# An RWKV recurrence with its products in fp16 high and low parts, and part of its vector work moved to ScalarE and GpSimd

## The reference

```python
low = jnp.tanh((x + delta * mu_x) @ W_x1).reshape(B, T, 5, PROJ_LR)
mus = jnp.einsum('blnr,dnr->blnd', low, W_x2) + x_bias
xr, xw, xk, xv, xg = [x + delta * mus[:, :, i] for i in range(5)]
r = (xr @ W_r)...; k = (xk @ W_k)...; v = (xv @ W_v)...; g = xg @ W_g
w = -jnp.exp(jnp.tanh(xw @ W_w1) @ W_w2 + b_w2)
def step(S, inp):
    o_t = jnp.einsum('bhk,bhkv->bhv', r_t, S) + jnp.einsum('bhk,hk,bhk,bhv->bhv', r_t, u, k_t, v_t)
    S = jnp.exp(w_t)[..., None] * S + k_t[..., :, None] * v_t[..., None, :]
o = ((o - mean) * jax.lax.rsqrt(var + EPS)).reshape(B, T, VAL_DIM)
o = (o * gn_w + gn_b) * (g * jax.nn.sigmoid(g))
return o @ W_o
```

## Time and profile before

| | |
|---|---|
| three runs | 1841.08, 1846.48, 1845.13 us |
| median | 1845.13 us |
| the profiled execution | 1845.41 us, of which 1843.6 us are its span |
| busy in the span | PE 1734.1, DVE 1442.4, ACT 1408.9, POOL 1431.1 us |
| mean granted clock of PE | 0.976 of full speed |

### The profile page before, as it was taken

The page is one execution under the profiler, slowest core; times in us unless marked ns, Lnnn a source line. Parts: engine busy times, 40 slices in busy tenths (PEclk is TensorE's granted clock), DMA queues, the critical chain, the costliest instruction groups (busy, mean ns, idle before and its releaser), DMA issues. The chain is left out here.

```text
span 1843.6 us, 54099 instructions
## 1 busy us (share of the span) xinstructions
PE 1734.1 (94%) x22920; PEld 1099.5 (60%) x22920; DVE 1442.4 (78%) x2658; ACT 1408.9 (76%) x1737; POOL 1431.1 (78%) x851
## 2 busy tenths in 40 slices
PE   5999999999999999999999999987899999978997
PEld 2466666666666666666666666675566666653454
DVE  5888888888888888888888887535888888855785
ACT  2688888888888888888888888943898888853464
POOL 6699999999999999999999999974765566634122
PEclk9899999999999999999999999998999999989999
DMA  5101010101011010101010100041111111100000
GB/s 141 27 20 31 19 31 22 28 25 29 24 27 26 25 31 19 31 23 28 23 31 19 28 20 9 2 157 29 40 41 37 37 37 37 33 25 2 1 0 23
DMA packets 71080, 57.02 MB, mean 31 GB/s; under 512 B 29196, under 2 KB 64184, under 8 KB 70840
## 3 DMA queue, kind: packets, MB, share of 16 engines
q1 hardware_dynamic: 70840, 53.57, 11.5%
HBM read 14.67 MB, written 1.05 MB: 9 GB/s over the span
## 5 line engine op out<-in xcount | busy, mean ns | idle before, releaser
L278 POOL TENSOR_TENSOR ah_probs_lo<-ah_probs,ah_probs_hi 128x1024 f16<-128x1024 f32 x512 | 1073.2, 2134 | 78.0 <-ACT ah_probs L487 77.9
L542 DVE TENSOR_REDUCE ah_part_max<-ah_p_m 128x1 f32<-128x512 f32 x1024 | 668.5, 685 | 121.5 <-PE ah_p_m L342 111.2
L484 ACT ACTIVATE ah_probs_hi<-ah_p_s 128x1024 f16<-128x1024 f32 x512 | 530.9, 1037 | 189.6 <-PE ah_p_s L358 178.4
L487 ACT ACTIVATE ah_probs<-ah_p_s 128x1024 f32<-128x1024 f32 x512 | 531.3, 1038 | 0.0
L372 PE MATMUL ah_p_o<-ah_v_hi,ah_probs_hi 128*128 128x65 f16 x4096 | 470.6, 195 | 5.7 <-POOL ah_probs_lo L278 5.1
L374 PE MATMUL ah_p_o<-ah_v_lo,ah_probs_hi 128*128 128x64 f16 x4096 | 470.6, 193 | 0.0
L376 PE MATMUL ah_p_o<-ah_v_hi,ah_probs_lo 128*128 128x65 f16 x4096 | 470.3, 194 | 0.0
L372 PEld LDWEIGHTS ah_p_o<-ah_v_hi,ah_probs_hi 128*128 128x128 f16 x4096 | 383.0, 98 | 84.4 <-DVE a_attn L565 12.2
L374 PEld LDWEIGHTS ah_p_o<-ah_v_lo,ah_probs_hi 128*128 128x128 f16 x4096 | 378.5, 98 | 91.3
L342 PE MATMUL ah_p_m<-ah_k_hi_lo,ah_q_hi_twice 128*128 128x512 f16 x1024 | 393.8, 385 | 6.6 <-DVE ah_part_max L542 3.5
L357 PE MATMUL ah_p_s<-ah_q_hi_twice,ah_k_hi_lo 128*128 128x512 f16 x1024 | 388.6, 380 | 0.8 <-ACT ah_probs L487 0.4
(11 more groups left out here) (316 smaller groups left out, 3083.4 us busy)
## 6 DMA issues: line engine op xcount, KB each, us to landing
ba_v_skew<-ba_v_own SPq DMA_DIRECT2D x64, 129.0 KB, 2.3
ah_q_hi_twice<-ah_hi SPq DMA_DIRECT2D x128, 64.0 KB, 2.0
ah_k_hi_lo<-ah_hi SPq DMA_DIRECT2D x64, 64.0 KB, 1.9
ah_one_k_hi<-ah_hi SPq DMA_DIRECT2D x64, 64.0 KB, 2.0
ah_k_hi_lo<-ah_lo SPq DMA_DIRECT2D x64, 64.0 KB, 2.0
ah_max_q_lo<-ah_lo SPq DMA_DIRECT2D x64, 64.0 KB, 2.0
ah_w_head<-in_w_heads SPq DMA_DIRECT2D x16, 160.0 KB, 2.5
bw_rot<-in_rot SPq DMA_DIRECT2D x4, 512.0 KB, 10.6
```

What stands on the lines that cost most here:

```text
L278: pool.tensor_tensor(pl[:, p % RW, :, :], pb[:, p % RP, :, :], ph[:, p % RW, :, :], ALU.subtract).then_inc(lo_pool, 1)
L484: act.activation(ph[:, p % RW, :, :], p_s[:, p % 2, :, :], ACT.Exp, scale=HD ** -0.5)
L487: act.activation(pb[:, p % RP, :, :], p_s[:, p % 2, :, :], ACT.Exp, scale=HD ** -0.5).then_inc(exp_done, 1)
L542: dve.tensor_reduce(part[:, t, 2 * half + b:2 * half + b + 1], p_m[:, b, :], AX, ALU.max).then_inc(maxed, 1)
```

## The change

- *Products.* The inputs of r, k and v are split into an f16 high part (ACT, `high_x`) and an f16 rest (POOL, `low_x`, into the memory of hT); so are the weights (POOL, four instructions ahead of the recurrence). A product is three f16 products into one bank: high by high, high by rest, rest by high. The tanh for the decay is made twice by weights laid out twice: the lower 64 partitions hold the high part, the upper 64 become the rest (`low_tw`, DVE), so that w takes two f16 products.
- *Splits.* `low_x` of chunk 0 stands in the mixing part, that of chunk c + 1 in the steps h = 0, 1, 2 of chunk c, each ahead of that step's bonus.
- *Bonus.* u*k*v is made by ACT (a copy with a factor per partition), added by POOL (`bonus`), and POOL makes the carry copy. DVE's scan takes its first value straight from the last column of the chunk before. DVE multiplies by r one step later (`weigh`), and so PE makes r(n - 1) and out(n - 2) in step n.
- *Norm of the outputs.* The mean is taken off within `out` (other constants in sel). ACT copies and squares (`centre`). The root is the exponential of minus half a logarithm, with one Newton step by DVE (four small instructions); logarithm and exponential are in one table, loaded once.
- *Places.* `turn_o` of a chunk moves from h = 3 of the next chunk to h = 0 of the one after it; `scale_o` and `norm_o` likewise to h = 0, `gate_o` to h = 1, `ln_root` to h = 3.

```diff
-                    pe.matmul(p_w[:, :], ww2[:, rs], tw[:, tok(c)], start=True, stop=True).then_inc(w_ready, 1)
+                    pe.matmul(p_w[:, :], w2_hi[:, rs], tw[:, tok(c)], start=True, stop=False)
+                    pe.matmul(p_w[:, :], w2_lo[0:P // 2, rs], tw[0:P // 2, tok(c)], start=False,
+                              stop=True).then_inc(w_ready, 1)
...
+                def three(out, k, n, ready):
+                    c, h = divmod(n, HCH)
+                    rs = slice(h * P, (h + 1) * P)
+                    pe.matmul(out, w_hi[:, k, rs], x_hi[:, k, tok(c)], start=True, stop=False)
+                    pe.matmul(out, w_hi[:, k, rs], x_lo[:, k, tok(c)], start=False, stop=False)
+                    pe.matmul(out, w_lo[:, k, rs], x_hi[:, k, tok(c)], start=False, stop=True).then_inc(ready, 1)
...
+                    three(p_kr[:, 0, :], K_COL, n, k_ready)
                     if n >= 1:
-                        out(n - 1)
-                    if h == 3 and c >= 1:
-                        turn_o(c - 1)
+                        receive(n - 1)
+                    if n >= 2:
+                        out(n - 2)
+                    if h == 0 and c >= 2:
+                        turn_o(c - 2)
                     if h == 1 and c >= 2:
                         out_y(c - 2)
+                receive(STEPS - 1)
+                out(STEPS - 2)
+                turn_o(CLAST - 1)
                 out(STEPS - 1)
...
+                    act.wait_ge(kv_done, n + 1)
...
+                    act.activation(ukv[:, n % 2, :], kv[:, n % 2, :], ACT.Copy,
+                                   scale=scols[:, 1, h:h + 1]).then_inc(ukv_done, 1)
+                    if h == 0 and c >= 2:
+                        scale_o(c - 2)
                     if h == 0 and c == CLAST:
                         norm(1, 0)
-                    if h == 1 and c >= 1:
-                        square(c - 1)
                     if h == 2 and c >= 1:
+                        centre(c - 1)
+                    if h == 3 and c >= 1:
                         root(c - 1)
...
+                for n in range(STEPS):
+                    c, h = divmod(n, HCH)
+                    if h == 0 and c >= 2:
+                        norm_o(c - 2)
+                    if h == 1 and c >= 2:
                         gate_o(c - 2)
-                    norm_o(c - 1)
-                    if c >= 2:
+                    if h < 3 and c < CLAST:
+                        low_x(c + 1, 2 - h)
+                    bonus(n)
+                    if c < CLAST:
+                        carry(n)
+                    if h == 3 and c >= 2:
                         ln_root(1, c - 2)
+                norm_o(CLAST - 1)
```

More of the change, by code:

```diff
@@ L1791, in _ @@
                 pe.wait_ge(z_ready, NCH)
[L1792 removed]
+                pe.wait_ge(w_lo_done, 2)
+                pe.wait_ge(tw_f32_done, NCH)
+                pe.wait_ge(tmp_ready, MIXES * NCH)
                 for n in range(STEPS):
@@ L1951, in _ @@
                 copy_x2(0)
-                square(CLAST)
+                centre(CLAST)
+                root(CLAST)
                 tanh_f(0, 0)
-                root(CLAST)
                 tanh_f(0, 1)
@@ L1999, in mix, with low_x, bonus, carry @@
                     pool.tensor_tensor(mixed_x, tmp[:, n % 2, :], xTp[:, xtok(c)], ALU.add).then_inc(mixed, 1)
+                def low_x(c, k):
+                    pool.wait_ge(mixed, MIXES * (c + 1))
+                    pool.wait_ge(x_hi_done, 3 * (c + 1))
+                    pool.tensor_tensor(x_lo[:, k, tok(c)], (x_r, x_k, x_v)[k][:, tok(c)], x_hi[:, k, tok(c)],
+                                       ALU.subtract).then_inc(x_lo_done, 1)
+                def bonus(n):
+                    c, h = divmod(n, HCH)
+                    pool.wait_ge(scanned, n + 1)
+                    if c >= 1:
+                        pool.wait_ge(carried, n - HCH + 1)
+                    if n >= 2:
+                        pool.wait_ge(pr_done, n - 1)
+                    pool.wait_ge(ukv_done, n + 1)
+                    pool.tensor_tensor(m[:, n % 2, :], ukv[:, n % 2, :], st[:, h, c % 2, 0:CH],
+                                       ALU.add).then_inc(m_done, 1)
+                def carry(n):
+                    c, h = divmod(n, HCH)
+                    pool.tensor_copy(st[:, h, (c + 1) % 2, 0:1], st[:, h, c % 2, CH:CH + 1]).then_inc(carried, 1)
                 def norm_o(c):
@@ L2019, in _ @@
                 pool.wait_ge(cleared, 2)
-                for c in range(NCH - 1):
-                    ln_root(0, c)
+                ln_root(0, 0)
+                ln_root(0, 1)
+                pool.wait_ge(late.scan_in, late.SCAN)
+                pool.tensor_copy(w_hi[:, :, :], w[:, :, :]).then_inc(w_hi_done, 1)
+                pool.tensor_copy(w2_hi[:, :], ww2[:, :]).then_inc(w_hi_done, 1)
+                ln_root(0, 2)
                 for c in range(NCH):
@@ L2147, in _ @@
                         if i == 2 and c >= 1:
+                            low_tw(c - 1)
                             gate_g(c - 1)
@@ L2153, in _ @@
                         delta_z(c + 2)
+                low_tw(CLAST)
                 gate_g(CLAST)
@@ L2193, in _ @@
                     dve.tensor_tensor(pr[:, n % 2, :], m[:, n % 2, :], p_kr[:, 1, :], ALU.mult).then_inc(pr_done, 1)
+                for n in range(STEPS):
+                    c, h = divmod(n, HCH)
+                    dve.wait_ge(v_done, n + 1)
+                    dve.wait_ge(k_ready, n + 1)
+                    if n >= 2:
+                        dve.wait_ge(ukv_done, n - 1)
+                    dve.tensor_tensor(kv[:, n % 2, :], p_kr[:, 0, :], v_sb[:, n % 2, :], ALU.mult).then_inc(kv_done, 1)
+                    dve.wait_ge(kv_done, n + 1)
+                    dve.wait_ge(dec_done, n + 1)
+                    first = st[:, h, 0, 0:1] if c == 0 else st[:, h, (c - 1) % 2, CH:CH + 1]
+                    dve.tensor_tensor_scan(st[:, h, c % 2, 1:], dec[:, n % 2, :], kv[:, n % 2, :], first, ALU.mult,
+                                           ALU.add).then_inc(scanned, 1)
+                    if n >= 1:
+                        weigh(n - 1)
                     if n == 0:
```

171 lines of the change are left out of this document (93 added, 78 removed).

## The result

The changed kernel takes 1849.62 us (median of 8 runs, 1847.89 to 1852.53) against 1846.42 for the kernel before (8 runs, 1841.08 to 1848.03). The ratio is 1.0023, with a 95% interval from 1.0013 to 1.0033: slower by a little, and within the 0.3% set as the bound. 1849 was predicted.

What follows compares the result with a forecast made beforehand. PE (TensorE) was taken to bound the recurrence at 4.33 us a step, with DVE close behind. The terms -8.4 + 2.7 + 0.9 + 3.6 + 3.4 + 1.3 = +3.5 us gave 1849 us, range 1836 to 1858.

Steps and rivals of the forecast that it cites:

- TensorE in chunks 0 and 1: Recurrence, first two chunks: f16 products cut most steps to 3.2 us, 26.65 against 35.01, minus 8.4 us.
- Chunks 2 and 3: Recurrence, last two chunks: three slower chains, 39.25 against 36.53 us, plus 2.7, and plus 0.9 for half-speed products.
- (a): Step 8: norm_o, transposes and scale_o of chunk 0 delay the next exponential and v; 4.1 us instead of 3.2.
- (b): Step 9: gate_o of chunk 0, behind the bonus and held by a scan, delays out_y and w; 6.05 us.
- (c): Step 12: statistics, ln_root, norm_o, transposes, scale_o, norm, exponential and v in a chain; the step takes 8.8 us.
- Mixing: Mixing of the inputs: low_tw, subtractions and f16 copies delay the first kv by 3.6 us; bounds 0.7 and 5.
- Tail: After the last pr: transposes ahead of the last out, and ACT work ahead of the first tanh; plus 3.4 and 1.3 us.
- The 3.4: Tail: chunk 2's transposes ahead of the last out make last pr to first gate product 7.35 us, from 3.97.
- the 1.3: Tail: ACT does centring, root and table load ahead of the first tanh; plus 1.3 us, bounds 0 and 2.
- the chains don't bind: First rival, chunk ends: they arrive in time, chunks 2 and 3 run like 0 and 1; 1837 us, chance 0.28.
- Half clock: Second rival, recurrence: PE's waits halve its clock, 6.3 us a step; two or three give 1855 to 1858; chance 0.18.
- scan and POOL exclude each other: Third rival, recurrence: steps with a subtraction take 3.7 us instead of 3.2, plus 4.5, 1853 us; chance 0.10.

Runs made afterwards that it cites:

- f32_products: The changed kernel with v, k and r each made by one f32 product again, splits made but not read; ratio 1.0040 to the kernel before.
- mixing_order: The changed kernel with low_tw behind all parts, one low_x moved a chunk later, and chunk 3's f16 copies ahead of the gate's tanh; ratio 0.9990 to the kernel before.
- all_moves: The changed kernel with the edits of both_moves, tail_order and mixing_order together; 1838.97 us, ratio 0.9951 to the kernel before.
- both_moves: The changed kernel with the edits of norm_late and norm_o_first together; ratio 0.9993 to the kernel before.
- norm_late: The changed kernel with only ACT's norm of tokens 0 moved from step 12 to behind the root of step 15; ratio 1.0007 to the kernel before.
- norm_o_first: The changed kernel with only POOL's norm_o of chunks 0 and 1 moved ahead of ln_root, to the end of h = 3; ratio 0.9988 to the kernel before.
- all_y_f32: all_y_later with v, k and r each made by one f32 product again; 1843.29 us, ratio 0.9985 to the kernel before.
- tail_order: The changed kernel with, behind step 15, chunk 2's norm_o ahead of ln_root and scale_o ahead of norm; ratio 1.0010 to the kernel before.
- bonus_on_dve: The changed kernel with the bonus back on DVE as one instruction, without ACT's copy and POOL's addition; ratio 1.0074 to the kernel before.
- all_y_later: all_moves with out_y of chunks 0 and 1 one step later and low_tw of two chunks behind the last gate; 1832.78 us, ratio 0.9923 to the kernel before.
- low_x_twice: The changed kernel with each low_x of the loop done once more into a tile nothing reads; ratio 1.0043 to the kernel before.

## Why the prediction came out right

*TensorE in chunks 0 and 1 (26.65 predicted, 27.16 measured).* Right in mechanism for the steps at PE's pace, and f32_products shows it. The step was mis-sized by 0.2: w's two products start 0.32 apart, not 0.22. The first step is shorter (2.54, it has no r and no out). That h = 2 took 3.96 (3.9) is luck. The prediction put the copy and the square of the outputs on ACT; in the trace DVE has no gap in this step (chosen rows of step 6):

```profile
1741.93 1.16 POOL L2056 TENSOR_TENSOR t_hT<-t_x_r,t_x_rkv_hi 128x512 f16<-128x512 f32 x1
1742.04 2.14 DVE L2270 TENSOR_TENSOR_SCAN t_state<-t_decay,t_state,t_kv 128x512 f32<-128x512 f32 x1
1744.19 0.60 ACT L1983 ACTIVATE t_v<-t_p_v 128x512 f32<-128x512 f32 x1
1744.68 0.67 DVE L2177 TENSOR_REDUCE t_ssq<-t_sq 128x64 f32<-128x512 f32 x1
1745.27 0.67 DVE L2266 TENSOR_TENSOR t_kv<-t_p_kr,t_v 128x512 f32<-128x512 f32 x1
```

The subtraction holds the scan, the sum of squares (0.6), which the prediction left out of DVE's work, stands behind it, and v was there at 1744.79, 0.48 ahead of kv(7). Where the same scan took 1.66 and 1.65 us (mixing_order, all_moves), the step took 3.52 and 3.51. h = 3 took 3.99 instead of 3.55, because the first operation of the Newton step takes 0.91 us while POOL adds the bonus, not 0.2 (0.18 in the tail, where POOL rests):

```profile
1747.18 0.66 DVE L2258 TENSOR_TENSOR t_pr<-t_m,t_p_kr 128x512 f32<-128x512 f32 x1
1747.35 1.27 POOL L2067 TENSOR_TENSOR t_m<-t_x_w,t_state 128x512 f32<-128x512 f32 x1 [1.88 <-DVE t_state L2270]
1747.76 0.91 DVE L2181 TENSOR_SCALAR t_g_tanh<-t_ssq 128x64 f32<-128x64 f32 x1
...
1802.93 0.18 DVE L2181 TENSOR_SCALAR t_g_tanh<-t_ssq 128x64 f32<-128x64 f32 x1
```

*Chunks 2 and 3 (40.15 with the clock, 40.70 measured).* The sum is right, with errors in its terms that cancel. (a) 3.98 for 4.1. (b) 5.11 for 6.05: gate_o got in ahead of the scan, not behind it; where it came behind, both_moves took 6.35. (c) 9.01 for 8.8, but for another reason in part: I put ACT's norm (1.65) on the path and half clock as 0.9 beside it; norm_late shows that norm lies beside w, v and k at half clock, which take as long. Step 13 took 4.51 instead of 2.7: the products for kv(14) were not already there, since PE, at half clock until 1776.1, began them at 1778.38. Step 11 took 4.86 (4.5) and the end from kv(15) 5.68 (5.15), both with the longer Newton step; h = 2 took 3.85 and 3.70 (4.0 and 3.95), again with DVE as the engine without a gap. The place of norm_o, which the prediction named as its weakest point, is shown by norm_o_first to be worth 4.9 us.

*Mixing (+3.6 predicted, +3.78).* Right, and chunk by chunk. Counted from the first z, x_g of the second, third and fourth chunk came 1.11, 2.32 and 3.19 us later than before, so these chunks lost 1.1, 1.2 and 0.9 (0.7, 1.3 and 0.9 predicted), and ACT's part behind them lost 0.6 (0.7). Both profiles had the lower clock in chunk 1's products. mixing_order took back 2.55 of the 3.78, and all_y_f32, at the same clock, stands at 52.12, 0.2 above the kernel before.

*Tail (+4.7 predicted, +3.52).* The late norm_o ahead of the last out is shown by tail_order: 3.92 instead of 6.88. The 3.4 came out as 2.9, the 1.3 as 0.6.

*The sum (+3.5 predicted, +3.62 in the profiles).* That it is within 0.1 us is luck: the four terms were off by +0.55, +0.57, +0.18 and -1.18 us, and the clock alone moves M by 1.5 us from profile to profile.

*The rivals.* That the chains don't bind is refuted: PE waits 4.72 us in (c). Half clock came behind (c), and at the first products of v and k ahead of kv(0) (0.59 to 0.63 each, granted clock 0.58 from 1719 to 1722 us); in chunks 0 and 1 it did not come. bonus_on_dve shows how near it is: a wait of 1.89 us stands in front of steps of 6.24 and 4.54 us instead of 3.07 and 3.40. That scan and POOL exclude each other is true, and was the cost that I left open between 0 and 1.1:

```profile
1753.84 1.26 POOL L2087 TENSOR_TENSOR t_oT<-t_o_scaledT,t_gate 128x512 f32<-128x512 f32 x1
1753.96 2.22 DVE L2270 TENSOR_TENSOR_SCAN t_state<-t_decay,t_state,t_kv 128x512 f32<-128x512 f32 x1
1755.07 2.07 POOL L2056 TENSOR_TENSOR t_hT<-t_x_k,t_x_rkv_hi 128x512 f16<-128x512 f32 x1
```

gate_o, 0.12 us ahead, keeps the scan until 1756.18 (2.22 instead of 1.28), and this scan keeps the next subtraction (2.07 instead of 1.16). So the rule of the Trainium skill, "SBUF — State Buffer", "Who interferes with whom", holds both ways round in this trace. But the price of 4.5 us did not come: steps 3 to 5 held such scans (1.72 to 1.90) and took 3.39 to 3.44, PE's own time. Of the steps of chunks 0 and 1 only step 6 was longer by a held scan, by some 0.4 us (an estimate from 3.96 and the 3.52 of mixing_order).

What stays open: which of the three moves in the mixing gives how much, and why the clock falls in some executions and not in others.

## What to carry to other kernels

When one engine gets faster, read what stood in the other engines' lists just early enough: here the gain of 7.85 us was lost to three places where a late instruction stood in front of a ready one, and came back (to 0.9923) by moving seven, without changing any work. After each move look where the wait went: with norm_o and norm both out of step 12 the wait moved to out_y in step 13, and it took the next move to cash both. A wait of TensorE costs twice, since the products behind it may run at half clock, so taking work off the engine that feeds it can be worth more than the sum of loads says: with the bonus back on DVE, A grew by 6.83 us, where the loads gave 1 to 2.

## What the runs showed of the hardware that was not expected

The same 24 products of the last `down`, behind the same wait of 1.98 us, took 2.94 us in nine of the fourteen profiles (before, after, all_y_later among them) and 4.57 to 4.58 in five (tail_order, all_moves, low_x_twice, f32_products, bonus_on_dve); the granted clock in them was 1.00 in the changed kernel and 0.63 in tail_order. In the same five, out_y of chunk 2, some 35 us earlier, had taken 1.77 to 1.92 us, and in the nine 1.05 to 1.27. Three of the five do not edit the tail. Such a step of 1.64 us can hide an edit worth 2 to 3.

Newton's first operation on DVE, with a single SBUF input (128x64), took 0.91 us instead of 0.18 beside a POOL addition that had begun, while pr, which reads one operand from PSUM, took its 0.66 beside such an addition. The Trainium skill, "SBUF — State Buffer", "Who interferes with whom", says that a tensor_scalar can take both ports; these rows agree.
